# Narrow attention: row products of two heads in a pair of banks, one maximum for both, and a new rule for who gets which bank

## The chip, the cores and the metric

The kernel runs on one core of a Trainium2 chip. Its engines are TensorE (PE, matmuls; PEld is its weight load), VectorE (DVE), ScalarE (ACT), GpSimd (POOL) and SyncE (SP, which issues the DMAs). Matmuls write to PSUM, which has eight banks of 512 fp32 values per partition. Each engine runs its own stream in order, and the streams wait for each other by semaphores. The metric is the device time of one execution in microseconds, as a median of runs.

## What is computed

Four blocks in a row on x (4 x 512 x 320) with a context (4 x 512 x 192). The diff touches only the attention of 20 heads of 16 values ("narrow"): the self- and cross-attention of the second block, and the cross-attention of the fourth.

```python
# second block (L1), for each of 4 batches
h1 = ln(x);  x = attn(h1, h1,  q1, k1, v1, o1_w, o1_b) + x
h2 = ln(x);  x = attn(h2, ctx, q2, k2, v2, o2_w, o2_b) + x
# fourth block (L3)
x = attn(x, ctx, Wq, Wk, Wv, Wo, bo) + x

def attn(x, c, wq, wk, wv, wo, bo):          # 20 heads of 16
    q, k, v = heads(x @ wq), heads(c @ wk), heads(c @ wv)
    sim = einsum('bhid,bhjd->bhij', q, k) * 16 ** -0.5
    out = einsum('bhij,bhjd->bhid', softmax(sim), v)
    return merge(out) @ wo + bo
```

The first block (L0) is attention of 20 heads of 64 ("wide") twice and a feed-forward layer; the second block ends with a feed-forward layer; the third (L2) is a gated attention over 32 tokens. None of these changes.

## The kernel before

**Stages.** One program goes through eight stages: s0 and s1 (wide attention, run `r0`), s2 (feed-forward), s3 and s4 (narrow self- and cross-attention, run `r3`, eight batches), s5 (feed-forward), s6 (gated), s7 (narrow cross-attention, run `r7`, four batches). By the trace the narrow steps lie from about 1784 to 2480 us and from about 2957 to 3291 us.

**A step of the narrow attention.** The 20 heads are five groups of four (u = 0 to 4), and the 512 keys or queries four blocks. A batch n is so 20 steps i = 4u + kb, written out for each engine in `narrow_steps_pe`, `narrow_steps_act` and `narrow_steps_dve`. For the softmax the kernel forms the scores twice:

- *Row products* (`rows_pe4`, L1072): queries by keys in bf16, one matmul of 512 columns for each of the four heads, each in a strip of 32 rows of the array. DVE takes the maximum of each row (`rows_dve4`, L1084) with its sign changed into `negm`. Row products run LEAD = 6 steps ahead of the rest, so those of a batch begin at step 14 of the batch before.
- `negm{u}` turns these maxima over by four PE transposes (L1107), and DVE adds them to the queries (L1115), in rows that the column products then sum over.
- *Column products* (`cols_pe`, L1059): keys by queries in fp32, four heads into banks 0 to 3 (`QUAD`). ACT takes their exponential, two heads at a time (L1097), into `probs`. The next step's column products wait for these two exponentials.

On PE a step is: row products of heads 0 and 1, column products of heads 2, 3, 0, 1, row products of heads 2 and 3, then the step's **large items**: one of Q, K, V (projections, L1251, L1276, L1302), mix (probabilities by values, L1126), turn and out (transposes, L1141, L1163), y (output projection, L1179), T and C (transposes of the inputs, L1204, L1231), and `negm`. ACT empties mix, out, T, C, Q, K and V, and DVE empties turn, negm and y. In a steady batch the large items of step i are: 0 Q2 V3; 1 mix4; 2 K2 negm1; 3 turn4 T0; 4 out0 out1 T1; 5 mix0; 6 out2 T2 negm2; 7 turn0 y0 (C0); 8 (C1) y1 y2; 9 mix1; 10 Q0 negm3; 11 turn1 y3; 12 K0; 13 mix2; 14 V0 negm4; 15 turn2 V1; 16 Q1; 17 mix3; 18 K1 negm0; 19 turn3 V2 (C0 and C1 in cross batches only). On ACT a step's two exponentials come ahead of its copies; on DVE its maxima come ahead of its other work.

**Who gets which bank.** Row products and large items share banks 4 to 7 (`NX`). The class `Turns` goes through all items ahead of time and gives each a bank by `choose`: before, the next of the four in turn (`len(self.place) % len(self.banks)`). An item's k-th use of a bank waits on PE until that bank's counter `free{bank}` is at k (`wait_free`); whoever empties the bank raises it. With four row products and one large item in a step, the large item gets the bank of the step's first row product. Two large items get those of the first and second, and so on. The joined steps (-1, while the feed-forward stage s2 ends) and the tail steps (beside s5) use the same functions.

Of the kernel before, what the change touches and what calls it, by code (L numbers as in the profile page):

```python
# [14 lines left out]
F32 = mybir.dt.float32  # L15
BF16 = mybir.dt.bfloat16
ALU = mybir.AluOpType
ACT = mybir.ActivationFunctionType
AX = mybir.AxisListType

P = 128
# [20 lines left out]
class Memory:  # L42


    def __init__(self, nc, ctx):
# [34 lines left out]
        self.bank = [self.pair[i // 2][:, i % 2, :] for i in range(6)]  # L80
        self.bank += [ctx.enter_context(nc.psum_tensor(f"bank{i}", [P, 512], F32)) for i in (6, 7)]
        self.PJ = self.bank[0:2]
# [5 lines left out]
        self.TR = self.bank[7]  # L88
        self.NX = self.bank[4:8]
        self.XB = self.bank[6:8]  # L90
# [22 lines left out]
def program(nc, io):  # L113
    with ExitStack() as ctx:
# [260 lines left out]
        class Turns:  # L375


            def __init__(self, name, stages, banks, steps, then=None, led=False):
                self.then, self.led = then, led
                self.work = [(s, b) for s in stages for b in range(B)]  # L380
                self.N = len(self.work)
                self.cross = [s.prm["cross"] for s, _ in self.work]
                self.sems, self.name, self.banks = {}, name, banks
                self.place, self.period, self.upto = {}, {}, {}
                count = [0] * len(banks)
                for n in range(-1, self.N + 1):
                    for i in range(steps):
                        for item in self.step_items(n, i):
                            bank = self.choose(item[0], i)
                            self.place[item] = (bank, count[bank])  # L390
                            self.period[item] = steps * n + i
                            count[bank] += 1
                        self.upto[steps * n + i] = tuple(count)

            def choose(self, name, i):
                return len(self.place) % len(self.banks)

            def sem(self, what):
# [11 lines left out]
            def wait_free(self, pe, item, n):  # L410

                bank, k = self.place[item, n]
                self.wait(pe, f"free{bank}", k)

            def wait_full(self, eng, item, n):
# [17 lines left out]
        def n_view(r, n):  # L433
            return V[r.work[n][0].name]
# [12 lines left out]
        class WideRun(Turns):  # L447

            wide = True
# [549 lines left out]
        def rows_items(r, n, i):  # L999

            n, i = n + (i + LEAD) // 20, (i + LEAD) % 20
            return [(f"row{i // 4}_{i % 4}_{h}", n) for h in range(4)] if 0 <= n < r.N else []

        class Run(Turns):

            wide = False

# [53 lines left out]

        def rows_pe4(pe, r, n, i, heads):

            for item, m in rows_items(r, n, i):
                u, qb, h = int(item[3]), int(item[5]), int(item[7])
                if h in heads:
                    v, strip = n_view(r, m), slice(32 * h, 32 * h + 32)
                    if qb == 0 and h == 0:
                        r.wait(pe, "q_cast", 5 * m + u + 1)
                        r.wait(pe, "k_cast", 5 * m + u + 1)  # L1070
                    r.wait_free(pe, item, m)
                    nc.tensor.matmul(r.bank_of(item, m)[:, :], v["QB"][strip, u, qb * P:qb * P + P], v["KB"][strip, u, :], start=True, stop=True  # L1072
                                     ).then_inc(r.full(item, m), 1)

        def rows_dve4(dve, r, n, i):

            for item, m in rows_items(r, n, i):
                u, qb, h = int(item[3]), int(item[5]), int(item[7])
                v = n_view(r, m)
                if qb == 0 and h == 0:  # L1080
                    r.wait_full(dve, f"negm{(2, 3, 0, 1, 4)[u]}", m if u in (2, 3) else m - 1)
                tile, at = (2, 16 - 16 * (h // 2)) if u == 4 else (u % 2, 16 - 16 * (u % 2))
                r.wait_full(dve, item, m)
                nc.vector.tensor_reduce(v["negm"][:, tile, qb, 32 * h + at:32 * h + at + 1], r.bank_of(item, m)[:, :], AX.X, ALU.max,  # L1084
                                        negate=True).then_inc(r.free(item, m), 1)

# [14 lines left out]
        def negm_pe4(pe, r, n, u):  # L1101
            v, item = n_view(r, n), f"negm{u}"
            r.wait_free(pe, item, n)
            for h in range(4):
                r.wait_out(pe, f"row{u}_3_{h}", n)
            for qb in range(TB):
# [157 lines left out]
        def Q_pool4(pool, r, n, c):  # L1264
            v = n_view(r, n)
            r.wait_full(pool, f"row{min(2 * c + 1, 4)}_3_3", n - 1)
            r.wait_out(pool, f"Q{c}", n)
# [22 lines left out]
        def K_pool4(pool, r, n, c):  # L1290
            v = n_view(r, n)
            r.wait_full(pool, f"row{min(2 * c + 1, 4)}_3_3", n - 1)
            r.wait_out(pool, f"K{c}", n)
# [33 lines left out]
        def narrow_steps_pe(pe, r, n, i0, i1):  # L1327
            now, new, old = 0 <= n < r.N, n + 1 < r.N, 0 <= n - 1
            feeds = new or now and r.then
            for i in range(i0, i1):  # L1330
                u, kb = i // 4, i % 4
                rows_pe4(pe, r, n, i, (0, 1))
                if now:
                    cols_pe(pe, r, n, i, (2, 3, 0, 1)).then_inc(r.sem("cols"), 1)
                rows_pe4(pe, r, n, i, (2, 3))
                if i == 0 and now:
# [891 lines left out]
```

## Time and profile before

| | us |
|---|---|
| median of 3 runs | 3327.07 (3326.29 to 3332.21) |
| profiled execution, its own time | 3336.34 |
| span of the profiled execution | 3334.6 |
| PE busy | 3214.7 (96%) |
| DVE busy | 1737.4 (52%) |
| ACT busy | 1476.5 (44%) |
| mean granted TensorE clock | 0.989 |

A busy PE means that a matmul was in flight: four matmuls in four strips at once count once, and the tail of one overlaps the next. So the share says how many holes there are in PE's stream, not how well the array is used. A wait of DVE, ACT or POOL costs nothing by itself. "Idle before" in a group's row is how long the engine stood before instructions of the group, with the one that ended the wait. The granted clock is a share of 2.4 GHz.

### The profile page before, as it was taken

How to read it: one execution, taken by the hardware profiler on the slowest of the kernel's cores; microseconds unless marked ns; L12 is line 12 of the kernel's file. 1: busy time of each engine (PE TensorE's matmuls, PEld its weight loads, DVE VectorE, ACT ScalarE, POOL GpSimd, SP SyncE). 2: the span in 40 equal slices, each digit the busy share in tenths (PEclk: the TensorE clock that was granted, in tenths of full speed). 3: DMA queues.
4: the chain of work that ended last, by engine and by line, in shares of the span. 5: the costliest groups of instructions: out<-in, count | busy, mean ns of one | idle time of the engine just before them, and what ended most of it. 6: DMA issues, size and time to landing. Idle time of an engine off the chain costs nothing.

```text
span 3334.6 us, 39289 instructions
## 1 busy us (share of the span) xinstructions
PE 3214.7 (96%) x15478; PEld 1462.8 (44%) x15478; DVE 1737.4 (52%) x2568; ACT 1476.5 (44%) x1983; POOL 805.1 (24%) x620
## 2 busy tenths in 40 slices
PE   7999999999999999999999999999999999989997
PEld 3344344443434343435444344444434545643443
DVE  2645455454555555552234677777762222656664
ACT  3544444445454545441112656666652112326664
POOL 2544444454554554550000000000000000000000
PEclk9999999999999999999999999999999999989999
DMA  3000000000100000000000000000002000000000
GB/s 110 24 16 20 16 17 20 23 19 20 58 18 18 17 23 13 16 24 20 0 5 26 1 1 1 30 11 6 1 23 65 1 0 33 1 5 6 14 9 17
DMA packets 37284, 62.32 MB, mean 19 GB/s; under 512 B 7024, under 2 KB 24944, under 8 KB 36208
## 3 DMA queue, kind: packets, MB, share of 16 engines
q1 hardware_dynamic: 37104, 59.82, 5.9%
q8 instruction: 125, 2.05, 0.3%
q14 instruction: 55, 0.45, 0.0%
HBM read 57.19 MB, written 2.62 MB: 18 GB/s over the span
## 4 chain that ended last, share of the span: by engine, by line
PE 89%; DVE 5%; ACT 4%; issue 1%; POOL 0%; DMA 0%; ACTq 0%; DVEq 0%; POOLq 0%
PE bank L1589 9%; PE bank L510 9%; PE bank L595 9%; PE bank L1126 7%; PE bank L737 5%; PE bank L351 5%; PE bank L673 5%; PE bank L1059 4%; PE bank L1251 3%; PE bank L676 3%; PE bank L709 3%; PE bank L1276 3%; PE bank L1179 2%; PE bank L533 2%; DVE heads L1084 2%; PE bank L1594 2%
## 5 line engine op out<-in xcount | busy, mean ns | idle before, releaser
L1084 DVE TENSOR_REDUCE heads<-bank 128x1 f32<-128x512 f32 x960 | 598.3, 683 | 237.2 <-PE bank L1072 236.4
L544 DVE TENSOR_REDUCE heads<-bank 128x2 f32<-128x1024 f32 x320 | 392.4, 1226 | 594.7 <-PE bank L533 594.7
L581 POOL TENSOR_TENSOR heads<-heads,probs 128x1024 f32<-128x1024 f32 x160 | 389.5, 2434 | 12.5
L567 ACT ACTIVATE probs<-bank 128x1024 f32<-128x1024 f32 x320 | 328.0, 1025 | 130.3 <-PE bank L519 130.0
L577 POOL TENSOR_TENSOR heads<-probs 128x1024 f32<-128x1024 f32 x80 | 190.7, 2384 | 712.8 <-ACT probs L567 712.8
L510 PE MATMUL bank<-heads 64*128 64x512 f32 x1280 | 335.7, 602 | 0.1
L1059 PE MATMUL bank<-heads 32*128 32x512 f32 x1920 | 296.8, 628 | 25.8 <-ACT weights L1097 10.9
L595 PE MATMUL bank<-probs,values 128*64 128x512 f32 x1280 | 294.0, 601 | 1.4 <-ACT nmT L558 1.0
L1589 PE MATMUL bank<-hT,weights 128*128 128x512 f32 x640 | 291.8, 606 | 1.5 <-issue 1.5
L1097 ACT ACTIVATE weights<-bank 128x1024 f32<-128x1024 f32 x236 | 228.8, 1022 | 96.0 <-PE bank L1059 93.9
L1652 ACT ACTIVATE ctx_in<-bank,b_col 128x512 f32<-128x512 f32 x80 | 55.1, 688 | 419.4 <-PE bank L1594 323.8
L1072 PE MATMUL bank<-heads 32*128 32x512 bf16 x960 | 214.6, 387 | 26.7 <-DVE heads L1084 7.4
L1269 POOL CAST heads<-heads 128x512 bf16<-128x512 f32 x60 | 35.6, 616 | 842.2 <-ACT heads L1260 842.2
L1671 DVE SCALAR_TENSOR_TENSOR mixed<-bank,b_col,ctx_in 128x512 f32<-128x512 f32 x80 | 60.1, 751 | 258.1 <-ACT ctx_in L1652 142.7
L1589 PEld LDWEIGHTS bank<-hT,weights 128*128 128x128 f32 x640 | 119.6, 192 | 165.3 <-issue 163.8
L1097 ACT ACTIVATE probs<-bank 128x1024 f32<-128x1024 f32 x164 | 159.0, 1022 | 62.6 <-PE bank L1059 61.9
L684 ACT COPY heads<-bank 128x512 f32<-128x512 f32 x160 | 93.7, 585 | 187.8 <-PE bank L673 167.7
L351 PE MATMUL bank<-weights,mixed 128*128 128x320 f32 x640 | 175.4, 432 | 0.0
L1072 PEld LDWEIGHTS bank<-heads 32*128 32x128 bf16 x960 | 63.7, 92 | 237.5 <-issue 112.1
L673 PE MATMUL bank<-hT,heads 128*128 128x512 f32 x320 | 161.7, 628 | 0.0
L595 PEld LDWEIGHTS bank<-probs,values 128*64 128x64 f32 x1280 | 85.2, 137 | 172.4 <-issue 168.1
L291 POOL TENSOR_SCALAR vare<-mv 128x4 f32<-128x4 f32 x24 | 4.7, 195 | 577.7 <-DVE mv L277 488.3
(205 smaller groups left out, 4868.9 us busy)
## 6 DMA issues: line engine op xcount, KB each, us to landing
heads<-in_wqk SPq DMA_DIRECT2D x40, 320.0 KB, 2.8
heads<-in_wqk SPq DMA_DIRECT2D x40, 256.0 KB, 2.6
weights<-in_L_xattn_w_ff SPq DMA_DIRECT2D x3, 1600.0 KB, 7.2
weights<-in_L_xattn_ff_w SPq DMA_DIRECT2D x3, 1600.0 KB, 7.1
ctx_in<-in_ctx SPq DMA_DIRECT2D x12, 384.0 KB, 3.7
weights<-in_L_xattn_qkv_q SPq DMA_DIRECT2D x2, 1632.0 KB, 7.4
weights<-in_L_xattn_wo SPq DMA_DIRECT2D x2, 1600.0 KB, 12.2
x_res<-in_x SPq DMA_DIRECT2D x4, 640.0 KB, 13.3
```

What stands on the lines that cost most here:

```text
L351: last = nc.tensor.matmul(M.bank[QUARTER[t]][:, 0:D], v["OT"][c][:, t * P:t * P + P], v["wo"][:, c, :], start=c == 0, stop=c == NF - 1)
L510: nc.tensor.matmul(cols[:, g, :], v["KT"][strip, U % 2, kb * P:kb * P + P], v["QT"][strip, U % 2, :], start=True, stop=False)
L544: nc.vector.tensor_reduce(v["negm"][:, U % 2, qb, :].rearrange("p (g k) -> p g k", g=2)[:, :, 0], M.ROWS[:, :, :], AX.X, ALU.max, negate=T ...
L567: nc.scalar.activation(v["probs"][:, kb, :, :], M.COLS[kb % 2][:, :, :], ACT.Exp, scale=float(r.work[n][0].prm["dh"]) ** -0.5).then_inc(r. ...
L581: nc.gpsimd.tensor_tensor(ps, ps, pr[:, k, :, :], ALU.add).then_inc(r.sem("part"), 1)
L595: last = nc.tensor.matmul(bank[64 * g:64 * g + 64, :], v["V"][:, kb, 2 * u + g, :], v["probs"][:, kb, g, :], start=kb == 0, stop=kb == TB - 1)
L673: last = nc.tensor.matmul(q[:, :], w[:, e, :], M.hT[:, e, :], start=False, stop=e == 1)
L1059: last = nc.tensor.matmul(M.QUAD[:, g, :], v["KT"][strip, u, kb * P:kb * P + P], v["QT"][strip, u, :], start=True, stop=True)
L1072: nc.tensor.matmul(r.bank_of(item, m)[:, :], v["QB"][strip, u, qb * P:qb * P + P], v["KB"][strip, u, :], start=True, stop=True).then_inc(r ...
L1084: nc.vector.tensor_reduce(v["negm"][:, tile, qb, 32 * h + at:32 * h + at + 1], r.bank_of(item, m)[:, :], AX.X, ALU.max, negate=True).then_ ...
L1097: nc.scalar.activation(v["probs"][g % slots][:, 2 * h:2 * h + 2, :], M.QUAD[:, 2 * h:2 * h + 2, :], ACT.Exp, scale=float(r.work[n][0].prm[ ...
L1589: last = nc.tensor.matmul(bank[:, :], v["w1"][:, j, 2 * part + e, :], M.hT[:, e, :], start=first and e == 0, stop=(not first) and e == 1)
```

## The change

- The last two banks become a pair like the others, and `NX` lists six places: banks 4, 5, 6, 7 and the pairs (4,5) and (6,7). `shares` says which places overlap, and `wait_free` waits for the counters of all of them (as they stand when the item's turn comes).
- Row products become two items a step. Item p = 0 is heads 0 and 1, before the column products; p = 1 is heads 2 and 3, behind them. Each is two matmuls into a pair and one signal at the second.
- DVE takes one maximum of 128 x 2 x 512 for each item: two results per partition, one release of the whole pair.
- `choose`: in step i, p = 0 gets pair i mod 2 and p = 1 the other. Large items get banks of pair i mod 2, the pair of p = 0: the first its first bank, the second its second bank, a third the first again.

```diff
-        self.bank += [ctx.enter_context(nc.psum_tensor(f"bank{i}", [P, 512], F32)) for i in (6, 7)]
+        self.pair.append(ctx.enter_context(nc.psum_tensor("bank6", [P, 2, 512], F32)))
+        self.bank += [self.pair[3][:, i, :] for i in range(2)]
...
-        self.NX = self.bank[4:8]
+        self.NX = self.bank[4:8] + self.pair[2:4]
...
+                            self.beside[item] = [(k, count[k]) for k in self.shares(bank)]
...
                 self.wait(pe, f"free{bank}", k)
+                for other, count in self.beside[item, n]:
+                    self.wait(pe, f"free{other}", count)
...
-            return [(f"row{i // 4}_{i % 4}_{h}", n) for h in range(4)] if 0 <= n < r.N else []
+            return [(f"row{i // 4}_{i % 4}_{p}", n) for p in range(2)] if 0 <= n < r.N else []
...
-            wide = False
+            wide, large = False, 0
+
+            def choose(self, name, i):
+
+                if name[0:3] == "row":
+                    self.large = 0
+                    return 4 + (i + int(name[7])) % 2
+                self.large = 1 - self.large
+                return 2 * (i % 2) + 1 - self.large
+
+            def shares(self, bank):
+                return ((4,), (4,), (5,), (5,), (0, 1), (2, 3))[bank]
...
+                r.wait_free(pe, item, m)
+                for g in range(2):
+                    strip = slice(64 * p + 32 * g, 64 * p + 32 * g + 32)
+                    last = nc.tensor.matmul(r.bank_of(item, m)[:, g, :], v["QB"][strip, u, qb * P:qb * P + P], v["KB"][strip, u, :], start=True, stop=True)
+                last.then_inc(r.full(item, m), 1)
...
+                out = v["negm"][:, tile, qb, :].rearrange("p (g k) -> p g k", g=4)[:, 2 * p:2 * p + 2, at]
                 r.wait_full(dve, item, m)
-                nc.vector.tensor_reduce(v["negm"][:, tile, qb, 32 * h + at:32 * h + at + 1], r.bank_of(item, m)[:, :], AX.X, ALU.max,
-                                        negate=True).then_inc(r.free(item, m), 1)
+                nc.vector.tensor_reduce(out, r.bank_of(item, m)[:, :, :], AX.X, ALU.max, negate=True).then_inc(r.free(item, m), 1)
...
-                rows_pe4(pe, r, n, i, (0, 1))
+                rows_pe4(pe, r, n, i, 0)
                 if now:
                     cols_pe(pe, r, n, i, (2, 3, 0, 1)).then_inc(r.sem("cols"), 1)
-                rows_pe4(pe, r, n, i, (2, 3))
+                rows_pe4(pe, r, n, i, 1)
```

In the rows of the order below, bank4 stands for the tensor of banks 4 and 5 (and after, bank6 for that of 6 and 7), bank0 for the column products' four; r3_free0 to r3_free3 are the counters of banks 4 to 7, and r3_free4 and r3_free5, after, those of the two pairs. L1072 is a row product before, L1091 after.

PE before, step i = 12 of a self-attention batch: rows, columns, rows, then K0 (L1276), and the next step up to its mix (L1126).

```order
L1059 MATMUL bank0<-heads 128x512 [waits r3_exp] x3
L1072 MATMUL bank6<-heads 128x512 [waits r3_free2]
L1072 MATMUL bank7<-heads 128x512 [waits r3_free3]
L1276 MATMUL bank4<-hT,weights 128x512 [waits r3_free0]
L1276 MATMUL bank4<-hT,weights 128x512 x2
L1072 MATMUL bank4<-heads 128x512 [waits r3_free1]
L1072 MATMUL bank6<-heads 128x512 [waits r3_free2]
L1059 MATMUL bank0<-heads 128x512 [waits r3_exp] x4
L1072 MATMUL bank7<-heads 128x512 [waits r3_free3]
L1072 MATMUL bank4<-heads 128x512 [waits r3_free0]
L1126 MATMUL bank4<-weights,values 32x512 [waits r3_exp,r3_free1]
```

PE after, the same place; K0 is L1295 and the mix L1145.

```order
L1077 MATMUL bank0<-heads 128x512 [waits r3_exp] x3
L1091 MATMUL bank6<-heads 128x512 [waits r3_free3,r3_free2,r3_free5]
L1091 MATMUL bank6<-heads 128x512
L1295 MATMUL bank4<-hT,weights 128x512 [waits r3_free4,r3_free0]
L1295 MATMUL bank4<-hT,weights 128x512 x2
L1091 MATMUL bank6<-heads 128x512 [waits r3_free3,r3_free2,r3_free5]
L1091 MATMUL bank6<-heads 128x512
L1077 MATMUL bank0<-heads 128x512 [waits r3_exp] x4
L1091 MATMUL bank4<-heads 128x512 [waits r3_free1,r3_free0,r3_free4]
L1091 MATMUL bank4<-heads 128x512
L1145 MATMUL bank6<-weights,values 32x512 [waits r3_exp,r3_free5,r3_free2]
```

The order of the work is the same; K0 waited for the counter of one bank, and now for the pair's (r3_free4) too.

PE before, step i = 4 of a batch: out0 and out1 (L1163), T1 (L1204), and the next step's row products.

```order
L1072 MATMUL bank7<-heads 128x512 [waits r3_free3]
L1163 MATMUL bank4<-ident,mixed 108x128 [waits r3_free2,r3_free0]
L1163 MATMUL bank4<-ident,mixed 108x128 x3
L1163 MATMUL bank4<-ident,mixed 106x128 [waits r3_free2,r3_free1]
L1163 MATMUL bank4<-ident,mixed 106x128 x3
L1204 MATMUL bank6<-ident,xn 106x128 [waits r3_free2]
L1204 MATMUL bank6<-ident,xn 106x128 x3
L1072 MATMUL bank7<-heads 128x512 [waits r3_free3]
L1072 MATMUL bank4<-heads 128x512 [waits r3_free0]
```

PE after, the same place; out is L1182 and T1 L1223.

```order
L1091 MATMUL bank6<-heads 128x512
L1182 MATMUL bank4<-ident,mixed 108x128 [waits r3_free2,r3_free4,r3_free0]
L1182 MATMUL bank4<-ident,mixed 108x128 x3
L1182 MATMUL bank4<-ident,mixed 106x128 [waits r3_free2,r3_free4,r3_free1]
L1182 MATMUL bank4<-ident,mixed 106x128 x3
L1223 MATMUL bank4<-ident,xn 106x128 [waits r3_free4,r3_free0]
L1223 MATMUL bank4<-ident,xn 106x128 x3
L1091 MATMUL bank6<-heads 128x512 [waits r3_free3,r3_free2,r3_free5]
L1091 MATMUL bank6<-heads 128x512
```

T1 had a bank of its own, emptied of a row product; now it follows out0 in the first bank (r3_free0), which ACT empties.

## Rows read from the trace of the kernel before

**Rows 1.** The page: span, and busy time of PE, share, instructions.

```profile
span 3334.6 us, 39289 instructions
PE 3214.7 (96%) x15478; PEld 1462.8 (44%) x15478; DVE 1737.4 (52%) x2568; ACT 1476.5 (44%) x1983; POOL 805.1 (24%) x620
```

**Rows 2.** Windows: length, busy per engine, granted clock, DMA share, GB/s.

```profile
300.00:400.00 100.00, 99.86 (x450) 42.25 (x448) 52.21 (x51) 47.61 (x64) 47.34 (x31) 1.00 0.06 17
1994.70:2085.40 90.70, 86.15 (x549) 38.47 (x548) 63.53 (x120) 54.02 (x65) 7.14 (x12) 1.00 0.00 1
3110.00:3195.00 85.00, 82.23 (x550) 36.61 (x547) 59.40 (x103) 54.32 (x67) 5.94 (x10) 1.00 0.03 9
1850.00:1860.00 10.00, 8.29 (x58) 2.29 (x62) 5.52 (x10) 3.89 (x5) 0.00 (x0) 0.83 0.00 0
```

**Rows 3.** Groups by line: busy us, mean ns, idle before and releasers.

```profile
L1084 DVE TENSOR_REDUCE heads<-bank 128x1 f32<-128x512 f32 x960 | 598.3, 683 | 237.2 <-PE bank L1072 236.4
L544 DVE TENSOR_REDUCE heads<-bank 128x2 f32<-128x1024 f32 x320 | 392.4, 1226 | 594.7 <-PE bank L533 594.7
L1059 PE MATMUL bank<-heads 32*128 32x512 f32 x1920 | 296.8, 628 | 25.8 <-ACT weights L1097 10.9 <-ACT probs L1097 8.5 <-ACT mixed L1097 6.4
...
L544 DVE TENSOR_REDUCE heads<-bank x320: 1225/1226/1229, 33.7 to 1471.2; 128x2 f32<-128x1024 f32 x160
```

**Rows 4.** Timeline of a plain step, i = 10: start, us, engine, line.

```profile
2039.94 0.39 PE L1072 MATMUL bank<-heads 32*128 32x512 bf16 x2
2039.94 1.24 PE L1059 MATMUL bank<-heads 32*128 32x512 f32 x8
...
2040.43 2.48 DVE L1084 TENSOR_REDUCE heads<-bank 128x1 f32<-128x512 f32 x4 [1.93 <-PE bank L1072]
...
2040.90 0.38 PE L1072 MATMUL bank<-heads 32*128 32x512 bf16 x2
...
2041.21 2.85 PE L1251 MATMUL bank<-hT,weights 108*128 108x512 f32 x6
```

**Rows 5.** Timeline of step i = 12, DVE and PE.

```profile
2049.73 0.48 DVE L1507 BATCH_NORM_STATS2 stats<-x_res 128x6 f32<-128x320 f32 x1
2050.13 2.46 DVE L1084 TENSOR_REDUCE heads<-bank 128x1 f32<-128x512 f32 x4
...
2050.86 1.13 PE L1276 MATMUL bank<-hT,weights 108*128 108x512 f32 x2 [0.82 <-DVE heads L1084]
```

**Rows 6.** Timeline of step i = 13, which starts at 2053.63.

```profile
2054.05 1.89 DVE L1084 TENSOR_REDUCE heads<-bank 128x1 f32<-128x512 f32 x3 [1.46 <-PE bank L1072]
...
2055.32 0.38 PE L1072 MATMUL bank<-heads 32*128 32x512 bf16 x1 [0.35 <-ACT heads L1286]
...
2055.64 0.64 PE L1126 MATMUL bank<-probs,values 128*32 128x512 f32 x4
```

**Rows 7.** Timeline of steps i = 4 and 5 (from 2012.54 and 2016.15).

```profile
2013.13 0.38 PE L1072 MATMUL bank<-heads 32*128 32x512 bf16 x1 [0.21 <-DVE heads L1084]
...
2014.47 1.94 ACT L1097 ACTIVATE mixed<-bank 128x1024 f32<-128x1024 f32 x2 [0.67 <-PE bank L1059]
...
2015.55 0.65 PE L1204 MATMUL bank<-ident,xn 128*106 128x128 f32 x4
...
2016.29 1.08 ACT L1171 COPY mixed<-bank 108x512 f32<-108x512 f32 x2
2016.57 1.48 DVE L1084 TENSOR_REDUCE heads<-bank 128x1 f32<-128x512 f32 x2 [0.48 <-PE bank L1072]
...
2016.94 0.38 PE L1072 MATMUL bank<-heads 32*128 32x512 bf16 x1 [0.40 <-ACT mixed L1171]
...
2018.42 0.64 PE L1126 MATMUL bank<-weights,values 128*32 128x512 f32 x4
```

**Rows 8.** Timeline of step i = 6 and the start of 7 (2025.03).

```profile
2024.43 0.66 PE L1107 MATMUL bank<-ident,heads 128*128 128x128 f32 x4
...
2025.18 0.59 ACT L1171 COPY mixed<-bank 106x512 f32<-106x512 f32 x1
...
2025.82 0.38 PE L1072 MATMUL bank<-heads 32*128 32x512 bf16 x1 [0.41 <-ACT mixed L1171]
```

More of the change, by code:

```diff
@@ L383, in __init__ @@
                 self.sems, self.name, self.banks = {}, name, banks
-                self.place, self.period, self.upto = {}, {}, {}
+                self.place, self.period, self.upto, self.beside = {}, {}, {}, {}
                 count = [0] * len(banks)
@@ L396, in choose @@
                 return len(self.place) % len(self.banks)
+            def shares(self, bank):
+                return ()
             def sem(self, what):
@@ L1001, in rows_items, with shares @@
             n, i = n + (i + LEAD) // 20, (i + LEAD) % 20
-            return [(f"row{i // 4}_{i % 4}_{h}", n) for h in range(4)] if 0 <= n < r.N else []
+            return [(f"row{i // 4}_{i % 4}_{p}", n) for p in range(2)] if 0 <= n < r.N else []
         class Run(Turns):
-            wide = False
+            wide, large = False, 0
[5 more added lines that the diff above has]
+                return 2 * (i % 2) + 1 - self.large
+            def shares(self, bank):
+                return ((4,), (4,), (5,), (5,), (0, 1), (2, 3))[bank]
             def step_items(self, n, i):
@@ L1060, in cols_pe, with rows_pe4 @@
             return last
[L1062 to L1073, printed above, removed]
+        def rows_pe4(pe, r, n, i, p):
+            for item, m in rows_items(r, n, i)[p:p + 1]:
+                u, qb = int(item[3]), int(item[5])
+                v = n_view(r, m)
+                if qb == 0 and p == 0:
+                    r.wait(pe, "q_cast", 5 * m + u + 1)
+                    r.wait(pe, "k_cast", 5 * m + u + 1)
+                r.wait_free(pe, item, m)
[3 more added lines that the diff above has]
+                last.then_inc(r.full(item, m), 1)
@@ L1075, in rows_dve4 @@
         def rows_dve4(dve, r, n, i):
-            for item, m in rows_items(r, n, i):
-                u, qb, h = int(item[3]), int(item[5]), int(item[7])
+            for p, (item, m) in enumerate(rows_items(r, n, i)):
+                u, qb = int(item[3]), int(item[5])
                 v = n_view(r, m)
-                if qb == 0 and h == 0:
+                if qb == 0 and p == 0:
                     r.wait_full(dve, f"negm{(2, 3, 0, 1, 4)[u]}", m if u in (2, 3) else m - 1)
-                tile, at = (2, 16 - 16 * (h // 2)) if u == 4 else (u % 2, 16 - 16 * (u % 2))
+                tile, at = (2, 16 - 16 * p) if u == 4 else (u % 2, 16 - 16 * (u % 2))
+                out = v["negm"][:, tile, qb, :].rearrange("p (g k) -> p g k", g=4)[:, 2 * p:2 * p + 2, at]
@@ L1103, in negm_pe4 @@
             r.wait_free(pe, item, n)
-            for h in range(4):
-                r.wait_out(pe, f"row{u}_3_{h}", n)
+            for p in range(2):
+                r.wait_out(pe, f"row{u}_3_{p}", n)
             for qb in range(TB):
@@ L1265, in Q_pool4 @@
             v = n_view(r, n)
-            r.wait_full(pool, f"row{min(2 * c + 1, 4)}_3_3", n - 1)
+            r.wait_full(pool, f"row{min(2 * c + 1, 4)}_3_1", n - 1)
             r.wait_out(pool, f"Q{c}", n)
@@ L1291, in K_pool4 @@
             v = n_view(r, n)
-            r.wait_full(pool, f"row{min(2 * c + 1, 4)}_3_3", n - 1)
+            r.wait_full(pool, f"row{min(2 * c + 1, 4)}_3_1", n - 1)
             r.wait_out(pool, f"K{c}", n)
```

## The prediction

> **What bounds the kernel now.** I read the page first: the profiled span is 3334.6 us and PE is busy for 96% of it, with every other engine near or under half [rows 1]. So the time is that of TensorE's stream, and a change counts by what it takes out of that stream or by the holes it leaves in it. Next I read the windows. In the wide attention PE has no holes worth the name (99.86 of 100 us). In the narrow attention, which this change touches, one batch of 20 steps takes 90.7 us (self-attention) or about 85 us (cross), and PE is shown busy for 86 of the 90.7 [rows 2]. That leaves at most 4.5 us in a batch that shorter waits could give back, and DVE (63.5 us) and ACT (54.0 us) have slack.
>
> A share of busy time doesn't say what a wait costs, so the next view is the timeline of a single step [rows 4]. A plain step starts at 2039.94 with two row products, runs the column products beside and behind them until 2040.90, then the other two row products, and at 2041.21 the large item (here Q0). DVE starts the first of its four maxima at 2040.43, 0.49 us after the step's start, and does one every 0.60 us (2.48 us for four, of which a single one lasts 0.68).
>
> **The change, part by part.**
>
> *Maxima on DVE.* Four reductions of 512 columns become two of 1024. The wide attention already does the 128x1024 form with two outputs per partition: 1225 to 1229 ns, median 1226, against 683 ns for 512 columns [rows 3]. Both read fp32 from banks, so I take 1.23 us. Four back to back take 2.48 us now; two will take 2.3 to 2.45 us. DVE saves 0 to 0.15 us a step, on an engine that is a third idle. That is worth something only where its queue makes the first maximum late.
>
> *Row products on PE.* Still four of 512 columns a step, in the same strips, with the same column products between them: nothing. Each now waits for up to three bank counters in place of one; PE's sequencer has time for that beside the column products, so I put it at nothing, with 0.05 us a step (12 us in all) as its upper bound, the distance between the end of a maximum and the start of the matmul that it released in [rows 4] (2041.12 to 2041.21, of which some is fixed).
>
> *What the large item waits for.* Before, items take the four banks in turn, so a step's large item gets the bank of the first row product alone: it needs one 0.68 us maximum to be over. After, it sits in the first pair of its step and waits for both heads, whose common maximum takes 1.23 us. The order rows show it: the K item waited for one counter and now waits for the pair's as well. The maximum can't start earlier (both products are issued together already), so it ends 1.23 - 0.68 = 0.54 us later, measured from the same start. How much of this reaches PE depends on the step. I went through the batch from 1994.7 to 2085.4, i being the step:
>
> - Plain steps, i = 0, 1, 2, 10, 14, 16, 18. The large item starts 1.27 us after the step without having waited. After: 0.49 + 1.23 + 0.06 = 1.78, so 0.50 late; over the seven, where the maximum starts 0.42 to 0.49 us in, 0.43 to 0.50. Sum 3.3 us.
> - Steps where DVE comes late from y, turn, statistics or the query add, i = 3, 8, 9, 11, 12, 15, 19. At i = 12 the first maximum starts only at 2050.13, behind the second y and a statistics operation, and K0 starts at 2050.86, having waited 0.82 us for it [rows 5]. These pay the whole 0.54. Sum 3.8 us.
> - i = 13 and 17: the fourth row product waits for ACT's evacuation until 2055.32 and the mix starts at 2055.64 [rows 6]. The pair's maximum (2054.05 + 1.23) is over by then. Zero.
> - i = 4 to 7. At i = 4 there are three large items, out0, out1 and T1, and the third falls back on the bank of the first: T1 must now wait until ACT has copied out0. In the trace T1 starts at 2015.55 and ACT, busy with the exponentials from 2014.47, is done with out0 at about 2016.88 [rows 7]. Since the delay of step 3 is absorbed by a wait for the exponentials here, step 4 gets 0.8 to 1.2 us longer, I take 0.9. At i = 6 it is out2, T2 and negm2: negm2 starts at 2024.43 and would wait for the copy that ends at 2025.77 [rows 8], so 1.4 us. Step 5 gives back: before, a row product waited 0.79 us for out0's copy and held up the column products (2016.15 to 2016.94), and the mix started 2.27 us into the step; after, p0 is in the other pair, free, and the mix starts at 0.42 + 1.29 = 1.71: -0.56. Step 7 gives 0.1 back likewise. Sum +1.6 us.
>
> Per batch 3.3 + 3.8 + 0 + 1.6 = 8.7 us. In the cross batches the same sum is 8.2 to 8.5, since K and V are shorter and some steps wait for the exponentials anyway.
>
> *How many batches.* 960 maxima [rows 3] are 240 steps, twelve batches in two runs (8 and 4). Eight batches are full ones: 8 x 8.5 = 68 us. The first of each run has no old work; its larger items are few and PE often waits for exponentials, so some 5 us each, and the six lead-in steps before it cost 0.54 each on most, 2.7 us: 15 us for both runs. The last of each has row products in 14 steps only: 6 us each, 12 in all. Sum 95 us. From this I take off what DVE's shorter queue gives in the late steps, 0.1 us in seven steps of twelve batches, 8 us. **+87 us**, nearly all as holes in PE's stream.
>
> By the profiled execution that is 3334.6 + 87 = 3421.6 us of span; it ran 9.3 us above the median (3336.34 against 3327.07), so the forecast for the median is 3327 + 87 = 3414, about 2.6% slower. The bound of the unknown wait (12 us) lies on the slow side.
>
> The trace shows that a 1024 reduction costs less than two single ones apart (1.226 against 2 x 0.683). The Trainium skill ("Advanced Engine Details and Errata", The Read-Write Bubble) advises large tiles of 512 or 1024 elements, and one instruction over several banks, to pay the gap between instructions once. By that rule alone the merged maximum is a gain, 480 x (1.366 - 1.226) = 67 us of DVE time at most, and all of it would come off the total only if DVE were the bound: 3260. The sum above turns on when the first bank comes free, and DVE's slack in [rows 2] speaks against it; its chance lies in the faster case below.
>
> **Rivals.**
>
> *Smaller loss.* Part of the delays runs into waits that are there anyway, as at i = 13 and 17, and only the plain steps and i = 4 to 7 lose: 3.3 + 1.6 = 4.9 us a batch, times about ten and a half, 51 us: 3378. For it: PE sat idle for 25.8 us in total before column products, most of it for exponentials [rows 3]. Against it: in the late steps the large item already waits for the very maximum that gets longer. 0.11.
>
> *The clock falls too.* Where PE had long holes in a narrow batch the granted clock fell: 1850 to 1860 shows PE at 8.29 us busy and a clock of 0.83, some of it spent at 1.2 in place of 2.4 GHz, while the steady batches, with about 5% holes, show 1.00 [rows 2]. After the change holes make up about 13% of a batch, most at i = 4 to 6. One such dip in each of eleven batches costs 10 x 0.17 = 1.7 us each, 19 us; several would cost 60. So 3433 to 3475. For i = 3 to 6 I count 0.5 + 0.5 + 0.9 + 0.4 + 0.5 + 0.9 = 3.7 us of holes in some 17 us, which is as thin as that stretch. Against it: they are broken up by work, none is over 1 us, and one dip a batch is cheap. The Trainium skill ("TensorE: Matmul & The Clock Gate", A second HAM failure mode: psum-queue depth-cycling) tells of a kernel whose frequent short idles between groups made the clock swing between its two levels; by that rule this rival is what happens, and the steady batches of this trace, with holes in every second step and a clock of 1.00, don't bear it out at 5% of holes. 0.16.
>
> *Faster.* The pair comes free before PE asks for it. Then the 0.50 and 0.54 vanish and what stays is the waits of single row products that go (0.6 us at i = 4 and 0.79 at i = 5 [rows 7], 0.79 at i = 7 [rows 8]), worth 1 to 2 us a batch: 10 to 24 us, 3303 to 3317. It decides at a pair maximum of 1.27 - 0.49 - 0.06 = 0.72 us; the same form takes 1.226 in the wide part. 0.05.
>
> *No change.* Delay and gain cancel, or the pairs' free counts are met early because PE reaches the large item later than now (for instance the sequencer's waits dominate both). 3327. That the banks are not shared as described is excluded by the order rows. 0.03.
>
> **How the numbers follow.** Forecast case 0.65 at 3414 (3400 to 3430), smaller loss 0.11, clock 0.16, faster 0.05, no change 0.03. The range 3385 to 3440 holds the first case, about a third of the second and two thirds of the third, its cheap end: 0.8. A measurement of this kernel can tell about 0.2% (7 us) from no change. Faster 0.05, same 0.03, slower 0.92.
>
> **What would show it.** In the trace after: the batch of 90.7 us becomes 98 to 99; PE waits for the DVE maximum before Q, K, V, mix and turn items, some 100 us in total; a maximum of 128x1024 at 1.22 to 1.23 us; T1 and negm2 of a steady batch wait over 0.6 us for ACT's copies of out0 and out2; the wide part, the feed-forward and the gated attention keep their lengths. The prediction is wrong if the 1024 form is much shorter here, if large items start 1.3 us into plain steps as now, or if the clock falls within steady batches.

## The result: 3.1% slower

The changed kernel takes 3432.44 us (median of 4 runs, 3432.21 to 3435.38) against 3329.64 us before (3326.29 to 3336.91, 4 runs): a ratio of 1.0308, 95% interval 1.0288 to 1.0327. The span of its profiled execution is 3430.6 us, 96.0 us longer than before. The forecast was 3414 us, in a range of 3385 to 3440.

First its page, the lines that answer to [rows 1] and [rows 3]:

```profile
span 3430.6 us, 39485 instructions
...
PE 3193.3 (93%) x15478; PEld 1461.3 (43%) x15478; DVE 1710.2 (50%) x2088; ACT 1477.2 (43%) x1983; POOL 807.1 (24%) x620
...
L1104 DVE TENSOR_REDUCE heads<-bank 128x2 f32<-128x1024 f32 x480 | 568.5, 1220 | 298.5 <-PE bank L1091 298.2
```

PE does the same 15478 matmuls. Its holes (stretches with no matmul in flight) were 3334.6 - 3214.7 = 120 us and are 3430.6 - 3193.3 = 237 us, while its busy time fell by 21 us: all of the longer span is waiting, and no work was added. DVE has 480 instructions less and 27 us less work, and it waits longer for PE than before (298.5 us against 237.2). The maximum of 1024 columns takes 1220 ns on the mean, as in the wide part.

The windows of a self-attention batch and a cross batch of the last stage (start and end, length, then busy time of PE, PEld, DVE, ACT and POOL, granted clock, DMA share, GB/s), beside the 90.70 and 85 us of [rows 2]:

```profile
2012.60:2111.90 99.30, 84.43 (x549) 38.02 (x548) 61.05 (x80) 54.15 (x65) 7.11 (x12) 1.00 0.00 1
3184.40:3277.70 93.30, 80.23 (x548) 36.18 (x544) 56.83 (x64) 54.60 (x67) 5.91 (x10) 1.00 0.02 8
```

8.6 and 8.3 us more in a batch, all of it holes, at the full clock.

The timeline of the plain step i = 10 (start, us, engine, line; L1091 row products, L1077 column products, L1104 maxima, L1270 is Q0), beside [rows 4]:

```profile
2062.55 0.39 PE L1091 MATMUL bank<-heads 32*128 32x512 bf16 x2
...
2063.05 2.36 DVE L1104 TENSOR_REDUCE heads<-bank 128x2 f32<-128x1024 f32 x2 [2.65 <-PE bank L1091]
...
2063.52 0.38 PE L1091 MATMUL bank<-heads 32*128 32x512 bf16 x2
...
2064.38 1.10 PE L1270 MATMUL bank<-hT,weights 108*128 108x512 f32 x2 [0.48 <-DVE heads L1104]
```

Up to 0.97 us the step is as before. The first maximum starts 0.50 us in, before 0.49. Q0 starts 1.83 us in and not 1.27, with an idle time of 0.48 us that ends with the maximum.

Step i = 12, beside [rows 5]:

```profile
2073.61 2.34 DVE L1104 TENSOR_REDUCE heads<-bank 128x2 f32<-128x1024 f32 x2
...
2074.97 0.67 PE L1295 MATMUL bank<-hT,weights 108*128 108x512 f32 x1 [1.45 <-DVE heads L1104]
```

The first maximum starts 1.44 us into the step, to the hundredth as before (2050.13 in a step from 2048.69); K0 starts 2.80 us in, before 2.17.

Step i = 11 has two large items, turn1 and y3 (L1141 and L1179 before, L1160 and L1198 after; PEld is the load of their weights). Before, then after:

```profile
2046.27 0.42 PEld L1141 LDWEIGHTS bank<-ident,ox 128*128 128x128 f32 x4 [0.50 <-DVE heads L1084]
2046.87 0.57 PEld L1179 LDWEIGHTS bank<-weights,mixed 108*128 108x128 f32 x3 [0.18 <-DVE heads L1084]
```

```profile
2069.99 0.63 PE L1160 MATMUL bank<-ident,ox 128*128 128x128 f32 x4 [0.74 <-DVE heads L1104]
2070.46 1.24 PE L1198 MATMUL bank<-weights,mixed 108*128 108x320 f32 x4
```

The steps start at 2044.43 and 2067.56, so turn1 starts 1.84 us in before and 2.43 after. But y3 waited for the second single maximum before (2.44 us in, 0.60 behind turn1), and after its bank is free together with turn1's: it starts 2.90 us in, 0.47 behind. So a second large item gives back a part of what the first one loses, and the step gets only 0.35 us longer.

Steps i = 4 and i = 6, from 2032.32 and 2042.16 (L1182 out, L1223 T, L1126 negm, L1190 ACT's copy of out), beside [rows 7, 8]:

```profile
2034.12 1.05 PE L1182 MATMUL bank<-ident,mixed 128*108 128x128 f32 x8 [0.19 <-issue]
...
2035.60 1.07 ACT L1190 COPY mixed<-bank 108x512 f32<-108x512 f32 x2
2036.24 0.40 PEld L1223 LDWEIGHTS bank<-ident,xn 128*106 128x106 f32 x4 [1.32 <-ACT mixed L1190]
2036.24 0.65 PE L1223 MATMUL bank<-ident,xn 128*106 128x128 f32 x4 [1.07 <-ACT mixed L1190]
```

```profile
2044.44 0.60 PE L1223 MATMUL bank<-ident,xn 128*106 128x128 f32 x4
2045.34 0.59 ACT L1190 COPY mixed<-bank 106x512 f32<-106x512 f32 x1
...
2045.98 0.66 PE L1126 MATMUL bank<-ident,heads 128*128 128x128 f32 x4 [0.94 <-ACT mixed L1190]
```

T1 and negm2 each stand about a microsecond behind ACT's copy of what was in the first bank. In the next step the column products start at once (2036.83), where they had waited 0.79 us.

### The profile page after: what moved, and what is told of

It reads as the page before. It is cut to its first block, busy times and chain, and to the rows that moved or that the text cites. A ratio compares the mean times of both kernels' runs of the same rounds, so it can differ in the third digit from the quotient of the medians.

```text
span 3430.6 us, 39485 instructions
## 1 busy us (share of the span) xinstructions
PE 3193.3 (93%) x15478; PEld 1461.3 (43%) x15478; DVE 1710.2 (50%) x2088; ACT 1477.2 (43%) x1983; POOL 807.1 (24%) x620
## 4 chain that ended last, share of the span: by engine, by line
PE 87%; DVE 7%; ACT 3%; issue 3%; POOL 0%; DMA 0%; DVEq 0%; ACTq 0%; POOLq 0%
PE bank L1608 8%; PE bank L517 8%; PE bank L602 8%; PE bank L1145 6%; PE bank L744 5%; PE bank L352 5%; DVE heads L1104 5%; PE bank L680 5%; PE bank L1077 4%; PE bank L1270 3%; PE bank L683 3%; PE bank L1295 3%; PE bank L716 3%; PE bank L540 2%; PE bank L1198 2%
## 5 line engine op out<-in xcount | busy, mean ns | idle before, releaser
L1104 DVE TENSOR_REDUCE heads<-bank 128x2 f32<-128x1024 f32 x480 | 568.5, 1220 | 298.5 <-PE bank L1091 298.2
L551 DVE TENSOR_REDUCE heads<-bank 128x2 f32<-128x1024 f32 x320 | 392.4, 1226 | 592.0 <-PE bank L540 592.0
L1077 PE MATMUL bank<-heads 32*128 32x512 f32 x1920 | 298.3, 626 | 16.0 <-ACT weights L1116 7.0
L1288 POOL CAST heads<-heads 128x512 bf16<-128x512 f32 x60 | 35.5, 613 | 898.2 <-ACT heads L1279 898.2
L1091 PE MATMUL bank<-heads 32*128 32x512 bf16 x960 | 186.5, 387 | 35.0 <-issue 17.5
L1091 PEld LDWEIGHTS bank<-heads 32*128 32x128 bf16 x960 | 51.9, 91 | 250.1 <-issue 228.9
```

The lines of the kernel that those rows point to most:

```text
L551: nc.vector.tensor_reduce(v["negm"][:, U % 2, qb, :].rearrange("p (g k) -> p g k", g=2)[:, :, 0], M.ROWS[:, :, :], AX.X, ALU.max, negate=T ...
L1077: last = nc.tensor.matmul(M.QUAD[:, g, :], v["KT"][strip, u, kb * P:kb * P + P], v["QT"][strip, u, :], start=True, stop=True)
L1091: last = nc.tensor.matmul(r.bank_of(item, m)[:, g, :], v["QB"][strip, u, qb * P:qb * P + P], v["KB"][strip, u, :], start=True, stop=True)
L1104: nc.vector.tensor_reduce(out, r.bank_of(item, m)[:, :, :], AX.X, ALU.max, negate=True).then_inc(r.free(item, m), 1)
```

## The experiments

My theory: the large item is late because the first pair comes free as one, after a maximum of 1.22 us (release theory). Rivals: the placement of the large items costs by itself; any merged maximum costs; the waits on the counters cost. In the cuts of code "..." stands for lines left out, and a line that starts with # or that is no code says the edit in words.

### The placement alone, with single maxima

```diff
 # in words
-    items row.._a (pair), row.._b (pair); one maximum each
+    items row.._0, _1 in the two banks of pair i mod 2, row.._2, _3 in those of the other; one maximum and one counter each
```

> The bank placement of the change alone: the pairs change places and large items go to the first pair, but each head's row product has its own bank counter and its own maximum of 512 columns. Release theory (the large item is late because the first pair comes free only after a 1.22 us maximum): only the third large items of i = 4 and 6 stay late, about 1.7 us in a full batch, so 10 to 20 us over the kernel before, near 3345 us. Placement theory (which bank the large items get is what costs): the time stays that of the changed kernel, near 3432 us.

Measured: 3349.97 us, ratio 1.0051 (1.0036 to 1.0066) to the kernel before. A self-attention batch is 92.1 us:

```profile
1994.30:2086.40 92.10, 85.42 (x553) 37.63 (x554) 63.49 (x120) 54.07 (x65) 7.12 (x12) 1.00 0.00 1
```

The plain step i = 10 is the old one: its first maximum starts 0.49 us in and Q0 1.28 us in (L1100 row products, L1118 maxima, L1285 Q):

```profile
2040.86 0.39 PE L1100 MATMUL bank<-heads 32*128 32x512 bf16 x2
...
2041.35 1.89 DVE L1118 TENSOR_REDUCE heads<-bank 128x1 f32<-128x512 f32 x3 [1.92 <-PE bank L1100]
...
2042.14 0.70 PE L1285 MATMUL bank<-hT,weights 108*128 108x512 f32 x1
```

The timeline of step i = 4 has the hole before T1 (L1238) behind ACT's copy of out0 (L1205) all the same:

```profile
2016.53 0.65 PE L1238 MATMUL bank<-ident,xn 128*106 128x128 f32 x4 [1.31 <-ACT mixed L1205]
```

So the placement costs 1.3 to 1.8 us a full batch and 17 us in all (3349.97 against the 3333.01 of the kernel before that was timed beside it), and the merging the rest: 1.0308 - 1.0051, some 85 us (82.5 by the two medians). The release theory stands; the placement theory is out as the main cause.

### Which of the two merged maxima costs

```diff
 # in words; first_single: heads 0 and 1
-    one pair item, one maximum of 128 x 2 x 512
+    two bank items, two maxima of 128 x 512
 # second_single: the same for heads 2 and 3 in place of 0 and 1
```

> The change with single maxima and single bank counters for heads 0 and 1 (the first pair), and the merged maximum kept for heads 2 and 3. Release theory: the large item again waits for one 0.68 us maximum, and nobody is pressed for the second pair, so the same time as with single maxima everywhere or 2 to 5 us less, near 3343 us. If any merged maximum costs, whichever pair it is in: half way, near 3390 us.

> The mirror image: merged maximum for heads 0 and 1, single ones for heads 2 and 3. Release theory: the whole loss stays, 3430 to 3437 us, and plain steps still start their large item 1.8 us in. Any-maximum theory: near 3390 us.

Measured, against the kernel before: with heads 0 and 1 single 3357.84 us, 1.0076 (1.0061 to 1.0091); with heads 2 and 3 single 3431.99 us, 1.0299 (1.0283 to 1.0314). The batch of the second:

```profile
2010.00:2109.40 99.40, 84.66 (x548) 38.84 (x548) 62.33 (x100) 54.21 (x66) 7.14 (x13) 1.00 0.00 1
```

99.4 us, the batch of the changed kernel. Nearly all of the loss by merging hangs on the first pair, the one that the large items go to. The merged second maximum gains nothing: the kernel is 8 us above the one with single maxima, where I had expected the same or a little less (the intervals just overlap at 1.0061 to 1.0066; the batches are 92.2 to 92.4 against 91.9 to 92.1 us). Its groups by line show that not even DVE gains:

```profile
L1118 DVE TENSOR_REDUCE heads<-bank 128x1 f32<-128x512 f32 x480 | 308.2, 684 | 239.6 <-PE bank L1100 239.6
L1115 DVE TENSOR_REDUCE heads<-bank 128x2 f32<-128x1024 f32 x240 | 292.4, 1218 | 14.7 <-PE bank L1100 14.3
```

308.2 + 292.4 = 600.6 us busy, beside 598.3 for the 960 single ones of [rows 3]: single maxima that stand back to back already overlap (they start 0.60 us apart, and one takes 0.68). The batches make up only some of the 8 us; where the rest lies is open.

### No third large item in a step

```diff
-                if i == 4 and feeds: items += [("T1", n + 1)]
-                if i == 6 and feeds: items += [("T2", n + 1)]
+                if i == 5 and feeds: items += [("T1", n + 1)]
+                if i == 9 and feeds: items += [("T2", n + 1)]
```

The same on PE and ACT.

> The changed kernel with no third large item in a step of the self-attention batches: T1 moves from step 4 to step 5, T2 from step 6 to step 9. The holes before T1 (about 1.0 us) and negm2 (about 0.95 us) go; exponentials then hold up the next column products for a part of that. Theory: 1.5 us less in each of eight full batches, 3415 to 3422 us, 10 to 17 us under the changed kernel. If the third items cost nothing: 3432 us.

Measured: 3420.24 us, 1.0267 (1.0250 to 1.0284), 12 us under the changed kernel; a batch is 97.4 us in place of 99.3, 1.9 us less where 1.5 were expected. The third items' holes were real and cost about what was said.

### What the waits on the counters cost

```diff
 # more_waits, in the kernel before: one more wait, on a count that is always reached already
+                other, count = self.extra[item, n]     # the bank two places on, its count so far less one
+                self.wait(pe, f"free{other}", count)
 # fewer_waits, in the changed kernel: no wait on a count that PE has waited for already
-                self.wait(pe, f"free{bank}", k)
-                for other, count in self.beside[item, n]:
-                    self.wait(pe, f"free{other}", count)
+                for other, count in [(bank, k), *self.beside[item, n]]:
+                    if count > self.seen.get(other, 0):
+                        self.wait(pe, f"free{other}", count)
+                        self.seen[other] = count
```

> The kernel before, with one more wait on a bank counter ahead of each row product and each large item of the narrow attention, on a count that is always reached already: ten waits in a step with one large item in place of five (the changed kernel has eight). It prices the waits alone. Release theory: 0 to 10 us over the kernel before. If the waits themselves explained the large items that start at 1.80 to 1.87 us in place of the 1.78 that I had worked out: 0.05 us a step, some 10 to 12 us, and with them an eighth of the loss.

> The changed kernel without the waits on bank counts that PE has waited for already, so that a large item and a pair of row products mostly have one wait, on the instruction itself, in place of two or three, of which the late one stood on a semaphore instruction of its own. In the changed kernel a late large item starts 0.10 us after the end of the maximum, before 0.05 us. Theory: 0.04 to 0.06 us less in the 14 steps of a batch in which the large item waits, 6 to 10 us in all, near 3423 us. Rival: waits cost nothing however they stand (as they did when reached already): 3430 to 3432 us.

Measured: waits that are reached already cost nothing: 3332.47 us, 1.0001 (0.9992 to 1.0010). Without the repeated waits the changed kernel takes 3418.61 us, 1.0260 (1.0245 to 1.0275), 14 us less than the changed kernel with its 1.0308, whose interval starts at 1.0288; 6 to 10 were expected. The timeline of its plain step i = 10, and the window of its batch:

```profile
2058.25 0.39 PE L1092 MATMUL bank<-heads 32*128 32x512 bf16 x2
...
2060.03 1.12 PE L1271 MATMUL bank<-hT,weights 108*128 108x512 f32 x2 [0.43 <-DVE heads L1105]
```

```profile
2008.60:2107.20 98.60, 84.79 (x549) 37.11 (x548) 61.04 (x80) 54.15 (x65) 7.11 (x12) 1.00 0.00 1
```

Q0 starts 1.78 us in, the number of the prediction, and not 1.83; K, V and others gain up to 0.09. A second wait is free where PE doesn't wait, and costs 0.05 to 0.09 us where it does: the late counter then stands on an instruction of its own ahead of the weight load. In the traces this is 0.70 to 0.78 us in each of the eight full batches, 6 us in all. The spans of the two profiled executions differ by 13.9 us (3430.6 and 3416.7), and much of the rest lies where this edit changes next to nothing: 3.7 us ahead of the first narrow step (1781.7 and 1778.0) and 2.6 us in the stretch of s5 and s6 (446.8 and 444.2 us from the last column product of `r3` to the first row product of `r7`), which had 6.8 us more at 1.2 GHz in the slower one. So 6 us are shown for the waits, and 14 is no price of them. Sets of executions differ without any edit too: the kernel before has medians from 3329.64 to 3333.01.

### The other pair

```diff
-                    return 4 + (i + int(name[7])) % 2
+                    return 4 + int(name[7])
...
-                return 2 * (i % 2) + 1 - self.large
+                return 3 - self.large
```

> The changed kernel with pairs that don't change places and large items on the second pair (heads 2 and 3, banks 6 and 7). The large item then waits for the second maximum, which ends about 1.15 us after the first: release theory says that plain steps start their large item 2.9 us in, and the whole is 1.0 to 1.1 us a step slower than the changed kernel in steps that were bound by the first maximum, 150 to 230 us in all, 3580 to 3660 us. If large items were not bound by the maximum ahead of them: no difference from 3432 us.

Measured, in a single run: 3797.73 us, 465 us over the kernel before and not 250 to 330. The plain step i = 10 starts Q0 2.96 us in, as expected:

```profile
2141.96 0.39 PE L1091 MATMUL bank<-heads 32*128 32x512 bf16 x2
...
2142.46 2.36 DVE L1104 TENSOR_REDUCE heads<-bank 128x2 f32<-128x1024 f32 x2 [5.47 <-PE bank L1091]
...
2144.92 1.53 PE L1270 MATMUL bank<-hT,weights 108*128 108x512 f32 x3 [1.61 <-DVE heads L1104]
```

What I had not priced is in its windows, a batch and two stretches of it:

```profile
2077.00:2206.00 129.00, 93.46 (x549) 42.70 (x548) 61.76 (x79) 54.40 (x65) 7.11 (x12) 0.92 0.00 1
2120.00:2150.00 30.00, 22.60 (x124) 10.09 (x122) 15.66 (x21) 10.38 (x12) 0.57 (x2) 0.89 0.00 0
2150.00:2180.00 30.00, 20.17 (x115) 10.12 (x116) 14.99 (x23) 11.44 (x14) 2.98 (x6) 0.92 0.00 1
```

The batch is 129 us in place of 99.3. 1.13 us in each of 20 steps would be 23 of these 30; and the granted clock is 0.92, so part of the batch ran at 1.2 GHz (20.5 us of it by the trace, which can have cost 10 us at most). With 35.5 us of holes in a batch in place of 14.9 the clock falls within steady batches, which it does neither before nor after the change (1.00 in both). That is the clock rival of the prediction, one step further out. Of the whole, an estimate from the mean clocks gives a bound: (1 - 0.946) x 3795.9 = 205 us were lost to the lower clock at most, against (1 - 0.986) x 3430.6 = 48 in the changed kernel. So up to 157 of the 365 us over the changed kernel can be the clock's own; how much of them it is, and how much are waits that follow from it, stays open. The longer wait itself is shown by the plain step, not by the 465 us.

### Work of DVE that frees no bank

If the large item hangs on the end of the first maximum, then what makes that maximum start late costs too: y's second add, the statistics and the norm, 0.6 to 1.0 us of them ahead of the maxima in six steps of a batch. They free no bank.

```diff
 # in rows_dve4, ahead of the maxima of heads 2 and 3 (in the changed kernel "1" in place of "2")
+                if item[7] in "2":
+                    run_late()
 # y's second add (but y1's), bn_stats, bn_aggr and norm_apply
-                (issued at once)
+                late.append(...)
```

> The kernel before, with DVE's work that frees no bank (second add of y, statistics, norm) put off until behind the maxima of heads 0 and 1 of the next step (y1 excepted). The release theory says that PE's large items hang on the first maximum's end; here that maximum starts at 0.42 to 0.7 us in place of 1.0 to 1.45 us at i = 8, 9, 11, 12, 15 and 19. Expected gain 0.3 to 0.9 us in these, about 3 us in a self-attention batch and 1.5 us in the others: 20 to 30 us, 3300 to 3310 us. If DVE's lateness costs nothing: 3329 us.

> The changed kernel with the same DVE work put off until behind the first maximum of the next step. By the release theory the late steps become plain ones (large item at 1.8 us in place of 2.3 to 2.8): 20 to 30 us under the changed kernel, 3402 to 3412 us, still 70 us over the kernel before.

Measured: the kernel before with this edit takes 3315.46 us, 0.9944 (0.9931 to 0.9958): **faster than both kernels**. The changed kernel with it takes 3395.70 us, 1.0196 (1.0182 to 1.0210), 37 us under the changed kernel, more than the 20 to 30 that I had expected and than the 19 us that its eight full batches are shorter; the rest is not taken apart. Of the first, the timeline of step i = 12 (L1094 maxima, L1291 is K0, L1200 y's second add, now between the maxima) and the window of a batch:

```profile
2036.92 0.39 PE L1072 MATMUL bank<-heads 32*128 32x512 bf16 x2
...
2037.58 1.28 DVE L1094 TENSOR_REDUCE heads<-bank 128x1 f32<-128x512 f32 x2
...
2038.31 1.56 PE L1291 MATMUL bank<-hT,weights 108*128 108x512 f32 x3
...
2038.77 0.48 DVE L1200 TENSOR_TENSOR x_res<-ysum,x_res 128x320 f32<-128x320 f32 x1
```

```profile
1984.00:2072.00 88.00, 86.03 (x549) 38.57 (x548) 63.63 (x120) 53.95 (x65) 7.27 (x12) 1.00 0.00 1
```

The first maximum starts 0.66 us in and not 1.44, K0 at 1.39 and not 2.17, and the batch is 88.0 us in place of 90.7. The gain is 17 us where I had expected 20 to 30: six of the batch's 20 steps gain 0.3 to 0.8 (3.0 in all), the cross batches only 1.9 and 1.3 us, and step 0 loses 0.4, where its first maximum starts 0.77 us in and not 0.44: the norm now stands between the maxima of step 19, whose second pair and turn3's reciprocal and product then run into step 0.

Last, the same with T1 and T2 moved as in the third experiment, in the old rotation of banks:

```diff
 # before_late, and
-                if i == 4 and feeds: items += [("T1", n + 1)]
-                if i == 6 and feeds: items += [("T2", n + 1)]
+                if i == 5 and feeds: items += [("T1", n + 1)]
+                if i == 9 and feeds: items += [("T2", n + 1)]
```

> The kernel before with DVE's work put off, and with T1 moved from step 4 to step 5 and T2 from step 6 to step 9, in the old rotation of banks. In steps 5 and 7 the second row product now waits 0.79 us for ACT's copy and holds up the column products; with one large item less ahead of them it is the third and fourth row products that wait for that copy, behind the column products. Expected 1 to 1.5 us less in each full batch than with the put-off work alone, 3300 to 3308 us. If that hole is only moved (the mix starts no earlier): 3315 us.

Measured: 3321.31 us, 0.9968 (0.9956 to 0.9980). Expected were 3300 to 3308 us, or 3315 if the hole was only moved. Self-attention batches are 87.9 to 88.0 us as without the move: in step 5 the second row product waits 0.59 us and not 0.79, but the column products start 0.90 us in, behind an exponential, and not 0.79. The hole was only moved. The 6 us by which this run stands above the other (the intervals overlap at 0.9956 to 0.9958) don't lie in the full batches, and what they are is open.

## Why the prediction was right

- **The mechanism and its size.** A large item waits for the pair, 0.50 us in plain steps and 0.54 in late ones. Measured: Q0 at i = 10 starts 0.56 us later, K0 at i = 12 0.63 us later; in the batch from 2012.6 the plain steps are 0.42 to 0.57 us longer, 3.5 us for the seven (3.3 expected). Steps 13 and 17, put at zero, got 0.05 us longer. PE's idle time that ends with the maximum adds up to some 94 us in the whole run, where "some 100" was the sign.
- **What the late steps pay.** All seven were put at 0.54 us. Steps 3, 8, 9 and 12 got 0.47 to 0.60 us longer, but 11, 15 and 19 only 0.35: there a second large item had waited for the second single maximum before and no longer does (step i = 11 above). They pay 3.2 us and not 3.8. This term was 0.6 us too large, and the others together were 0.4 too small, with the cost of the waits in them. That the batch came out so well is in part luck.
- **i = 4 to 7.** Expected +0.9, -0.56, +1.4, -0.1. The step lengths of after less those of before (means over the six full batches of `r3`) are +0.89, -0.51, +1.38 and -0.06.
- **The batch.** 8.7 us expected, 99.3 - 90.7 = 8.6 measured; cross 8.2 to 8.5 expected, 8.0 to 8.4 measured.
- **The sum.** 95 us before the last term. By the starts of the batches in the two traces the span's 96.0 us lie so: 66.8 in the eight full batches (68 expected), 17.6 in the lead-ins and first batches of both runs (15), 9.7 in the last ones (12), together 94.1. The other 1.9 are 2.2 us less ahead of the first narrow step and 4.1 us more in the stretch of s5 and s6, which the change doesn't touch (442.7 and 446.8 us from the last column product of `r3` to the first row product of `r7`); after had 6.8 us more at 1.2 GHz there. The medians differ by 102.8 and not by 96: the profiled execution of before stood 6.7 us above its median of four. In the later experiments the kernel before has medians of 3332.2 to 3333.0, and the loss by these is 99 to 100 us.
- **The last term.** The step that failed is "what DVE's shorter queue gives in the late steps", -8 us. It is nothing: two merged maxima do take 0.12 us less than four single ones (2.36 and 2.48), but at i = 12 the first maximum starts 1.44 us in, before and after, and in the other late steps too it starts within 0.01 us of where it did. What makes it late is DVE's other work ahead of it (y, statistics, the query add, norm), not the queue of maxima: `before_late`, which puts some of that work off, gets it to 0.66. I took it off without a row. It is most of what parts the forecast of 87 from the spans' 96.0.
- **The waits.** Put at nothing with 12 us as bound, on the slow side. They cost 6 us in the full batches (`fewer_waits`), so putting them at nothing was wrong too. They don't come on top of the 95, for the 66.8 us of the full batches hold them already: there they are set off by what the late steps don't pay. That a time of 3432.44 is still in the range is owed to its slow side, which had been left open for this wait.
- **Clock.** Steady batches kept 1.00, and the window from 1850 to 1860 shows 0.85 after and 0.83 before. But in the first batch of the run the clock is down in two windows where it had not been; windows of before, then of after:

```profile
1820.00:1840.00 20.00, 17.35 (x94) 7.65 (x98) 13.02 (x21) 13.09 (x16) 1.23 (x2) 1.00 0.00 0
1860.00:1880.00 20.00, 18.70 (x115) 7.47 (x114) 13.80 (x25) 12.44 (x15) 2.35 (x4) 1.00 0.00 1
```

```profile
1820.00:1840.00 20.00, 16.74 (x74) 7.13 (x66) 9.97 (x9) 10.95 (x13) 1.23 (x2) 0.83 0.00 1
1860.00:1880.00 20.00, 17.55 (x104) 6.31 (x98) 11.03 (x14) 10.48 (x13) 1.17 (x2) 0.90 0.01 1
2860.00:2880.00 20.00, 19.54 (x105) 15.55 (x104) 5.93 (x20) 5.43 (x12) 0.00 (x0) 0.86 0.39 137
```

  20 x (0.17 + 0.10) = 5.4 us at most in the first batch, and 20 x 0.14 = 2.8 in the last line's window, between the two runs. Over the whole span the records of the clock have 101 us at 1.2 GHz after and 77 before, so 12 us of the 96 at most. So the clock rival came in places that it didn't name and at an eighth of the loss at most, and `second_pair` shows that it was near in the steady batches. Not all of this need come of the change: the kernel before has executions with mean clocks from 0.988 to 0.991.
- **Large tiles, and frequent idles.** The advice of the Trainium skill to use large tiles ("Advanced Engine Details and Errata", The Read-Write Bubble) holds for DVE's busy time where all maxima are merged: 480 of 1024 columns cost 568.5 us where 960 of 512 cost 598.3. It came out as no gain in the time of the kernel. The clock passage of the Trainium skill's "TensorE: Matmul & The Clock Gate" (A second HAM failure mode: psum-queue depth-cycling), frequent idles that let the clock swing, agrees with the 0.92 of `second_pair` and not with the 1.00 of the changed kernel's steady batches.

## What to carry to other kernels

Before merging two small instructions that free a buffer, ask who takes the buffer next: if the next taker needs the first half only, merging delays it by what the second half adds (0.54 us here) in nearly every round, even when the merged instruction is cheaper and its engine idle a third of the time. Merge only the half that nobody is waiting for, and expect little of it unless that engine is the bound. And on the engine that frees a buffer, put work that frees nothing behind work that does: here this alone was worth 0.56%.

## What the runs showed of the hardware

- A wait on a semaphore whose count is reached already cost PE nothing even five times a step (1.0001). A wait that is really late costs, and where it stands matters: after the maximum's end the matmul starts 0.05 us later where the wait stands on the weight load itself (before, i = 12: 2050.80 to 2050.86) and 0.10 us later where it stands on a semaphore instruction ahead of it (after, i = 9: 2058.88 to 2058.98).
- Two maxima of 128x1024 back to back start 1.13 us apart (2.36 us for two) where a single one takes 1.22 us; those of 128x512 start 0.60 us apart where one takes 0.68. So merging saves 0.07 us for each pair of maxima that stand back to back, and 1.366 - 1.226 = 0.14 only for ones that stand apart.
- TensorE's clock stayed at 2.4 GHz through batches of 99.3 us with 14.9 us of holes, none over 1.5 us, and was at 1.2 GHz for a part of the batches of 129 us with 35.5 us of holes, none over 2.6 us (mean 0.92).
